# A fused four-layer kernel: TensorE's loops written out, and each scan state's own products set ahead of those with the state before it

## The chip, the cores and the metric

The kernel runs on one core of a Trainium2 chip, as one launch. The metric is the device time of that launch in microseconds. The engines are TensorE (PE: matmuls; PEld: its weight loads), VectorE (DVE), ScalarE (ACT), GpSimd (POOL) and SyncE (SP, which here only issues DMAs). They run their own instruction streams side by side and are held together by semaphores alone.

## The reference

Four layers with residual sums over `x` of 128 x 64 x 1024 (batch, channels, time), float32:

```
x = x + einsum('bct,bcd->bdt', x, W0[cond])                 # per-sample channel mix
x = x + mask1 * (causal_conv(x, K1) + x * D1)               # SSM layer 1
x = x + (x @ W2.T + bias) + scale * ((x @ A[id].T) @ B[id].T)   # 1024 x 1024 on the time axis, with adapters
m = mask3 * x
x = x + mask3 * (causal_conv(m, K3) + m * D3)               # SSM layer 3
# K[h, l] = 2 Re sum_n Ct[h, n] exp(dtA[h, n] * l),  l < 1024, 64 modes n per channel h
```

Since K is a sum of 64 complex modes, a causal convolution can be split: within a chunk of 256 steps it is a small Toeplitz product ("near"), and everything older reaches a chunk through a state of 128 real numbers for each channel and sample ("far"). The state behind chunk k is the chunk's own contribution plus the decayed state behind chunk k-1.

## The kernel before, in words

**Stages.** Stage 0 (about the first 240 us) loads x in four units `i` of two blocks of 128 time steps, makes the channel mix with float32 matmuls (line 618), and writes the result to a scratch in DRAM. Between its matmuls stand the transposes of the weights (602) and the sums for the convolution kernels (586). DVE and ACT take the sums out, SP issues the loads of x, ACT the stores.

Then come 16 groups `g` of four channels (heads `h`, HG = 4, NG = 16). Values are split into a high and a low float16 half, and each product is made of three matmuls: high x high, high x low, low x high. In `body(g, more1)` PE does, in this order: `stage2(g)` (lines 737 to 753, the 1024 x 1024 layer with the adapters), then, interleaved, the scan states and the first convolution of group g+1 (`states(0, g+1, k)`, `near1`, `far1`) and the scan states of the third layer of group g (`states(1, g, k)`), and last the third layer's convolution of group g (`near3`, `far3`). The last group has no group behind it and a shorter order.

**The states.** `states(v, g, k)` makes the sums of the state behind chunk k (k = 0, 1, 2) of layer v (0: first, 1: third) in one PSUM bank: for each of four heads six matmuls of 128 columns from the chunk's own values (line 675), and for k > 0 three more from the halves of the state behind chunk k-1 (line 679). ACT then makes the high half of the sum (`state_hi`, line 1055) and DVE the low half (`state_lo`, line 1457), with the semaphores `st_hi[v]` and `st_lo[v]`. Banks are 7, 6, 7 for v = 0 and 4, 5, 4 for v = 1, so k = 2 writes over the bank of k = 0. For k > 0 the waits for both halves and for the decay table (`v_lo`) stand ahead of all 36 matmuls of the state.

**What sets the order.** Everything is written out by hand in the order in which each engine's program stands; there is no scheduler. PE's program has two loops with a counter in a register: `Fori(1, NBLK // 2)` over units 1 to 3 of stage 0 (line 644) and `Fori(1, NG - 1)` over groups 1 to 14 (line 852). Unit 0 and groups 0 and 15 are written out. Inside a loop, semaphore targets that depend on the counter are computed by register instructions. The other engines have loops of their own and are not touched.

Other lines that the steps name: DVE's 1472 (`take_conv1`, the masked take-over of the first convolution), 1499 (`lowf`, the adapters' low-rank sums scaled) and 1502 (their low half), 1509 (`lo3`, low half of the third layer's input), 1557 (the masked take-over of the third layer), ACT's 1110 (`outt`, its sums taken out), POOL's 531 and 534 (`past_of`, the third layer's input put together again from transposed halves), 507 to 521 (`make_tables`).

Of the kernel before, what the change touches and what calls it, by code (L numbers as in the profile page):

```python
# [35 lines left out]
B, C, T = 128, 64, 1024  # L36
NBLK = T // P
# [9 lines left out]
HG = 4  # L47
NG = C // HG
TB = 16
CHUNK = TB * TB  # L50
NCH = T // CHUNK
# [16 lines left out]
def at_least(engine, semaphore, value):  # L68

    if not (isinstance(value, int) and value <= 0):  # L70
        engine.wait_ge(semaphore, value)


def build(nc, x, ids0, len1, ids2, len3, w0, ssm1, ssm3, w2, bias2, lora_a, lora_b, lora_s, out):
    with ExitStack() as ctx:
        def sem(name):
            return ctx.enter_context(nc.semaphore(name))
# [12 lines left out]
        ps = ctx.enter_context(nc.psum_tensor("ps", [P, 8, 512], F32))  # L90
# [86 lines left out]
        vd = (vd1, vd3)  # L177
        ut = (ut1, ut3)
        st = ((s1[:, 0], s1[:, 1]), (s3h, s3l))
# [97 lines left out]
        v_lo = sem("v_lo")  # L277
# [4 lines left out]
        st_hi = [sem(f"st_hi{v}") for v in range(2)]  # L282
        st_lo = [sem(f"st_lo{v}") for v in range(2)]
# [41 lines left out]
        def made(v, g):  # L325

            if v == 0:
                return 2 * g - 1 if isinstance(g, int) and g else (0 if isinstance(g, int) else 2 * g - 1)
            return 2 * NG - 1 if isinstance(g, int) and g == NG - 1 else 2 * g + 2
# [228 lines left out]
        def _(pe):  # L558
# [3 lines left out]
            for dgroup in range(8):  # L562
                for e in range(8):
                    for q in range(2):
                        mm = nc.tensor.matmul(ps[q * C:(q + 1) * C, dgroup, e * PAIRS:(e + 1) * PAIRS], src[:, 8 * dgroup + e, :],  # L565
                                              onehot[:, :].rearrange("i (n q) -> i q n", q=2)[:, q, :], start=True, stop=True)
# [39 lines left out]
            def stage0(i, first):  # L606
                for m in range(2 * STEPS):
                    n = 2 * STEPS * i + m
                    s = m % NXH
                    k, step, odd = m // STEPS, m % STEPS // 2, m % 2  # L610
                    blk = 2 * i + k
                    l = m // 2
                    if not odd:
                        pe.wait_ge(x_loaded[l % NXIN], 16 * (STEPS // NXIN * i + l // NXIN + 1))

                    at_least(pe, (s0_even_out, s0_odd_out)[odd], STEPS * i + m // 2 - 1)
                    for j in range(GPAIRS):
                        mm = nc.tensor.matmul(ps[:, s, j * P:(j + 1) * P], xin[:, l % NXIN, j, odd * P:(odd + 1) * P],  # L618
                                              pick[:, l * GPAIRS + j, :], start=True, stop=True)
                    mm.then_inc(s0_summed, 1)  # L620
                    if not odd:
                        continue
                    if first and k == 0:
                        if step == 1:
                            turn_params()
                        if step == 3:
                            turn_lot(LOT_A)
                        if step == 5:
                            turn_lot(LOT_B)
                    else:  # L630
                        if step == 2:
                            sum_k(blk - 1)
                        if first and step == 3:
                            turn_lot(LOT_W)
                        if first and step == 6:
                            turn_lot(LOT_W + 1)
                        if not first and k == 0 and step == 3:
                            turn_lot(blk + LOT_W, 0)
                        if not first and k == 0 and step == 7:
                            turn_lot(blk + LOT_W + 1, 1)  # L640

            pe.wait_ge(iota_done, 5)
            stage0(0, True)
            with pe.Fori(1, NBLK // 2) as i:
                stage0(i, False)
            pe.wait_ge(s0_even_out, NBLK * STEPS // 2)
            pe.wait_ge(s0_odd_out, NBLK * STEPS // 2)
# [4 lines left out]
            def states(v, g, k):  # L652

                bank = ((7, 6, 7), (4, 5, 4))[v][k]
                if k == 0:
                    pe.wait_ge(u_turned[v], 32 * (g + 1))
                    if v == 0:
                        pe.wait_ge(x1_hi, HG * (g + 1))
                        pe.wait_ge(x1_lo, HG * (g + 1))
                    else:  # L660
                        pe.wait_ge(x3_hi, NBLK * (g + 1))
                        pe.wait_ge(x3_lo, NBLK * (g + 1))
                else:
                    pe.wait_ge(st_hi[v], (NCH - 1) * g + k)
                    pe.wait_ge(st_lo[v], (NCH - 1) * g + k)
                    pe.wait_ge(v_lo, made(v, g) + 1)
                if v == 0 and k == 1:

                    at_least(pe, s2_out, NBLK * g)
                hi, lo = x_of[v]  # L670
                for h in range(HG):
                    o = ps[:, bank, h * B:(h + 1) * B]
                    for q, (part, xx) in enumerate([(0, hi), (0, lo), (1, hi)]):
                        for blk in range(2):
                            mm = nc.tensor.matmul(o, ut[v][:, part, 2 * h + blk, :], xx[:, h, 2 * k + blk, :],  # L675
                                                  start=(q == 0 and blk == 0), stop=(k == 0 and q == 2 and blk == 1))
                    if k:
                        for q, (part, ss) in enumerate([(0, 0), (0, 1), (1, 0)]):
                            mm = nc.tensor.matmul(o, vd[v][:, part, h, (2, 0)[v], :], st[v][ss][:, h, k - 1, :], start=False, stop=(q == 2))  # L679
                mm.then_inc(st_summed[v], 1)  # L680

            def near1(g, h):

                b0 = conv1_bank(g, h)
                early = isinstance(g, int) and g == 0
                if h == 0:
                    pe.wait_ge(g1_turned, g + 1)
                if early or h == 0:
                    pe.wait_ge(x1_hi, HG * g + h + 1 if early else HG * (g + 1))
                    pe.wait_ge(x1_lo, HG * g + h + 1 if early else HG * (g + 1))  # L690
                if early:

                    if h == 2:
                        pe.wait_ge(k_scaled, NBLK - 1)
                    if h == 3:
                        pe.wait_ge(c1_out, 1)
                elif h < 2:

                    at_least(pe, c3_out, HG * (g - 1))
                else:  # L700
                    pe.wait_ge(c1_out, HG * g + h - 1)
                for bank in range(2):
                    for d in range(2):
                        for q, (part, xx) in enumerate([(0, x1h), (0, x1l), (1, x1h)]):
                            o = ps[:, b0 + bank, :].rearrange("p (k b) -> p k b", k=4)
                            m = xx[:, h, 4 * bank:4 * bank + 4, :]
                            if d:
                                o = o.rearrange("p (k two) b -> p k two b", two=2)[:, :, 1, :]
                                m = m.rearrange("p (k two) b -> p k two b", two=2)[:, :, 0, :]
                            nc.tensor.matmul(o, g1[:, h, part, d * P:(d + 1) * P], m, start=(d == 0 and q == 0), stop=False)  # L710
# [110 lines left out]
            def body(g, more1):  # L821
                stage2(g)
                if more1:
                    states(0, g + 1, 0)
                    near1(g + 1, 0)
                    states(0, g + 1, 1)
                    near1(g + 1, 1)
                    states(1, g, 0)
                    states(0, g + 1, 2)
                    states(1, g, 1)  # L830
                    far1(g + 1, 0)
                    states(1, g, 2)
                    far1(g + 1, 1)
                    for h in range(2, HG):
                        near1(g + 1, h)
                        far1(g + 1, h)
                    for h in range(HG):
                        near3(g, h)
                        far3(g, h)
                else:  # L840
                    near3(g, 0)
                    states(1, g, 0)
                    near3(g, 1)
                    states(1, g, 1)
                    states(1, g, 2)
                    for h in range(HG):
                        if h >= 2:
                            near3(g, h)
                        far3(g, h)

            body(0, True)
            with pe.Fori(1, NG - 1) as g:
                body(g, True)
            body(NG - 1, False)


        @block.scalar
# [740 lines left out]
```

## Time and profile before

| | |
|---|---|
| median of 3 runs | 1691.71 us (1690.57 to 1693.37) |
| the profiled execution | 1686.25 us, its span 1684.4 us |
| mean granted TensorE clock | 0.978 of full speed |
| PE / PEld / DVE / ACT / POOL busy | 93 / 61 / 61 / 31 / 49% of the span |
| stage 0 and what precedes the groups | 0 to 279.7 us |
| 15 groups, 0 to 14 | 279.7 to 1597.0 us |
| the last group | 1597.0 to 1684.4 us |

The profile is of one execution. Its page gives busy times and shares; the trace behind it gives each instruction with the idle time of its engine ahead of it and what ended that idle time ("<-DVE gbuf L1457": a semaphore from DVE's line 1457; "<-issue": nothing that the profile can name). Matmuls are pipelined, so the duration of a merged row contains the latency of its last matmul (about 0.16 us), and the next row starts before it ends. Times in the rows are counted from the start of the span. Line numbers of rows are those of the kernel before.

### The profile page before, as it was taken

The numbers are of one execution on the slowest core, as the hardware profiler recorded it, in microseconds if no ns is written. First come the engines' busy times: TensorE is split into PE (matmuls) and PEld (weight loads), VectorE is DVE, ScalarE is ACT, GpSimd is POOL, SyncE is SP. The second block draws the span as 40 slices with busy tenths as digits, with TensorE's granted clock in tenths as the row PEclk, the third lists the DMA queues.
The fourth block names the chain that finished last, engine by engine and source line by source line (L and its number), as shares of the span: only waits on it lengthen the run. The fifth ranks groups of instructions, "written<-read, shape, count | busy, mean of one in ns | idle before, by whom it ended". The sixth has DMA issues, their size and how long they took to land.

```text
span 1684.4 us, 30702 instructions
## 1 busy us (share of the span) xinstructions
PE 1572.3 (93%) x12183; PEld 1028.3 (61%) x12183; DVE 1033.4 (61%) x1345; ACT 528.5 (31%) x674; POOL 822.0 (49%) x365
## 2 busy tenths in 40 slices
PE   6777767999999999999999999999999999999996
PEld 6776654474747475656566665656574747474744
DVE  7787775656575656565655565656566665656532
ACT  4444431332323232232323232323232323232211
POOL 2000032438292928384746556555556574738434
PEclk9989879999999999999999999999999999999998
DMA  7799957253534444352526253535352626262314
GB/s 226 270 353 338 359 206 198 44 129 83 100 102 93 107 87 122 72 137 59 150 47 158 52 141 68 137 72 137 67 142 52 147 52 142 67 142 62 83 47 100
DMA packets 425956, 216.82 MB, mean 129 GB/s; under 512 B 337144, under 2 KB 412416, under 8 KB 423872
## 3 DMA queue, kind: packets, MB, share of 16 engines
q1 hardware_dynamic: 409728, 176.67, 42.1%
q10 hardware_dynamic: 16192, 39.67, 6.4%
q8 instruction: 23, 0.38, 0.1%
q14 instruction: 13, 0.11, 0.0%
HBM read 94.19 MB, written 71.76 MB: 99 GB/s over the span
## 4 chain that ended last, share of the span: by engine, by line
PE 83%; DVE 7%; DMA 6%; issue 3%; ACT 1%; POOL 0%; POOLq 0%; DVEq 0%; SPq 0%; ACTq 0%
PE ps L745 39%; PE ps L784 7%; PE ps L675 7%; DMA arena<-in_x_dram 5%; PE ps L710 5%; PE ps L737 5%; PE ps L753 5%; PE ps L797 4%; PE ps L679 3%; PE ps L618 3%; PE ps L727 2%; PE ps L723 1%; PE ps L565 1%; DVE arena L1355 1%; DVE arena L1509 1%
## 5 line engine op out<-in xcount | busy, mean ns | idle before, releaser
L745 PE MATMUL ps<-arena,w2t 128*128 128x512 f16 x3072 | 681.3, 379 | 0.0
L745 PEld LDWEIGHTS ps<-arena,w2t 128*128 128x128 f16 x3072 | 300.4, 98 | 362.3
L531 POOL TENSOR_TENSOR arena<-arena 128x1024 f32<-128x1024 f16 x64 | 150.8, 2356 | 551.7 <-DMA arena<-arena 534.0
L1515 DVE TENSOR_SCALAR arena<-ps,biasx 128x512 f32<-128x512 f32 x128 | 94.4, 748 | 204.0 <-ACT arena L1079 203.8
L1079 ACT ACTIVATE arena<-ps,biasx 128x512 f16<-128x512 f32 x128 | 87.1, 687 | 421.1 <-PE ps L753 421.1
L507 POOL TENSOR_TENSOR arena<-arena 128x1024 f32<-128x1024 f32 x32 | 73.0, 2280 | 288.4 <-DMA arena<-tab_scratch 226.4
L618 PE MATMUL ps<-arena 128*128 128x128 f32 x1024 | 145.3, 305 | 49.1 <-DMA arena<-in_x_dram 27.1
L618 PEld LDWEIGHTS ps<-arena 128*128 128x128 f32 x1024 | 136.8, 217 | 55.4 <-issue 24.3
L710 PE MATMUL ps<-arena 128*128 128x512 f16 (+1 forms) x768 | 138.2, 331 | 8.1 <-DVE arena L1434 8.1
L784 PE MATMUL ps<-arena 128*128 128x256 f16 (+1 forms) x1536 | 138.4, 247 | 3.2 <-DVE arena L1509 3.0
L534 POOL TENSOR_TENSOR arena<-arena,one_xs 128x1024 f32<-128x1024 f32 x64 | 135.2, 2112 | 5.0
L1509 DVE TENSOR_TENSOR arena<-arena 128x512 f16<-128x512 f32 x128 | 136.0, 1073 | 0.0
L784 PEld LDWEIGHTS ps<-arena 128*128 128x128 f16 x1536 | 124.0, 98 | 14.4 <-issue 3.5
L1557 DVE COPY_PREDICATED arena<-past,arena 128x1024 f32<-128x1024 uint8 x64 | 91.5, 1432 | 59.5 <-POOL arena L534 42.3
L710 PEld LDWEIGHTS ps<-arena 128*128 128x128 f16 x768 | 74.8, 99 | 59.3 <-issue 11.4
L1465 DVE SCALAR_TENSOR_TENSOR arena<-gbuf,arena 128x1024 f16<-128x1024 f32 x64 | 104.7, 1637 | 1.2 <-ACT arena L1013 1.2
L675 PE MATMUL ps<-arena 128*128 128x128 f16 x1152 | 88.8, 220 | 13.5 <-DVE gbuf L1457 5.1
L517 POOL TENSOR_TENSOR arena<-arena 128x1024 f32<-128x1024 f32 x32 | 99.9, 3123 | 2.5
L753 PE MATMUL ps<-gbuf,bt 128*128 128x512 f16 x384 | 101.2, 379 | 0.0
L675 PE MATMUL ps<-arena,gbuf 128*128 128x128 f16 x1152 | 88.2, 220 | 8.5 <-issue 7.0
L1457 DVE SCALAR_TENSOR_TENSOR arena<-ps,arena 128x512 f16<-128x512 f32 x48 | 33.2, 692 | 96.5 <-ACT arena L1055 96.5
L737 PE MATMUL ps<-arena,at 128*128 128x512 f16 x384 | 87.6, 385 | 4.8 <-DVE arena L1477 4.8
(213 smaller groups left out, 2156.3 us busy)
## 6 DMA issues: line engine op xcount, KB each, us to landing
arena<-in_x_dram SPq DMA_DIRECT2D x64, 512.0 KB, 8.0
out_dram<-arena SPq DMA_DIRECT2D x64, 512.0 KB, 3.0
gbuf<-x_scratch SPq DMA_DIRECT2D x120, 256.0 KB, 3.7
arena<-krow_scratch SPq DMA_DIRECT2D x32, 512.0 KB, 4.5
x_scratch<-arena ACTq DMA_DIRECT2D x14, 1024.0 KB, 9.3
x_scratch<-arena ACTq DMA_DIRECT2D x14, 896.0 KB, 8.6
arena<-tab_scratch SPq DMA_DIRECT2D x32, 200.0 KB, 2.6
w2t<-in_L_cond_weight_dram ACTq DMA_DIRECT2D x8, 512.0 KB, 3.5
```

The lines of the kernel that those rows point to most:

```text
L517: ptt(v4, v4, m4, ALU.add).then_inc(v_made, 1)
L531: nc.gpsimd.tensor_tensor(past[:, h % 2].rearrange("p (k t) -> p k t", k=NBLK), x3t[:, h % 2, 0], x3t[:, h % 2, 1], ALU.add).then_inc(past ...
L534: nc.gpsimd.tensor_tensor(past[:, h % 2], past[:, h % 2], one_xs[:, :].to_broadcast([P, T]), ALU.mult).then_inc(past_ready, 1)
L618: mm = nc.tensor.matmul(ps[:, s, j * P:(j + 1) * P], xin[:, l % NXIN, j, odd * P:(odd + 1) * P], pick[:, l * GPAIRS + j, :], start=True, s ...
L675: mm = nc.tensor.matmul(o, ut[v][:, part, 2 * h + blk, :], xx[:, h, 2 * k + blk, :], start=(q == 0 and blk == 0), stop=(k == 0 and q == 2 ...
L710: nc.tensor.matmul(o, g1[:, h, part, d * P:(d + 1) * P], m, start=(d == 0 and q == 0), stop=False)
L737: mm = nc.tensor.matmul(ps[:, 7, :], at[:, part, k, :], xx[:, :, k, :], start=(k == 0 and q == 0), stop=(k == NBLK - 1 and q == 2))
L745: nc.tensor.matmul(ps[:, 4 + o % 3, :], w2t[:, o, part, k, :], xx[:, :, k, :], start=(k == 0 and q == 0), stop=False)
L753: mm = nc.tensor.matmul(ps[:, 4 + o % 3, :], bt[:, part, o * P:(o + 1) * P], xx, start=False, stop=(q == 2))
L784: nc.tensor.matmul(ps[:, bank, c0:c0 + n], xx[:, h, j, :], g3[:, h, part, g0:g0 + n], start=(j % 4 == 0 and xx is x3h and part == 0), stop ...
L1465: stt(x1l[:, h], x1f[:, h], XS / FS, x1h[:, h], ALU.mult, ALU.subtract).then_inc(x1_lo, 1)
L1509: tt(x3l[:, :, o, :], x3f[:, o % 2], x3h[:, :, o, :], ALU.subtract).then_inc(x3_lo, 1)
```

## The change

It touches PE's program alone, in three places. The loop over units 1 to 3 and the loop over groups 1 to 14 are written out, so that counters, branches and register instructions go and every semaphore target is a constant. In `states` the own products of all four heads now come first, and for k > 0 the waits for the halves of the state before and for the decay table stand behind them, ahead of the twelve matmuls that read them. For k = 2 a wait of its own stands ahead of the own products: that the low half of k = 0 was made, whose bank they write over. Since the four heads' sums are now open in one bank together, only the first matmul of a state has `start`. Matmuls, their number and their operands stay as they are.

```diff
             stage0(0, True)
-            with pe.Fori(1, NBLK // 2) as i:
+            for i in range(1, NBLK // 2):
                 stage0(i, False)
...
-                else:
-                    pe.wait_ge(st_hi[v], (NCH - 1) * g + k)
-                    pe.wait_ge(st_lo[v], (NCH - 1) * g + k)
-                    pe.wait_ge(v_lo, made(v, g) + 1)
+                elif k == 2:
+
+                    pe.wait_ge(st_lo[v], (NCH - 1) * g + 1)
                 if v == 0 and k == 1:
 
                     at_least(pe, s2_out, NBLK * g)
...
                             mm = nc.tensor.matmul(o, ut[v][:, part, 2 * h + blk, :], xx[:, h, 2 * k + blk, :],
-                                                  start=(q == 0 and blk == 0), stop=(k == 0 and q == 2 and blk == 1))
-                    if k:
+                                                  start=(h == 0 and q == 0 and blk == 0), stop=(k == 0 and q == 2 and blk == 1),
+                                                  skip_group_check=True)
+                if k:
+                    pe.wait_ge(st_hi[v], (NCH - 1) * g + k)
+                    pe.wait_ge(st_lo[v], (NCH - 1) * g + k)
+                    pe.wait_ge(v_lo, made(v, g) + 1)
+                    for h in range(HG):
+                        o = ps[:, bank, h * B:(h + 1) * B]
                         for q, (part, ss) in enumerate([(0, 0), (0, 1), (1, 0)]):
-                            mm = nc.tensor.matmul(o, vd[v][:, part, h, (2, 0)[v], :], st[v][ss][:, h, k - 1, :], start=False, stop=(q == 2))
+                            mm = nc.tensor.matmul(o, vd[v][:, part, h, (2, 0)[v], :], st[v][ss][:, h, k - 1, :], start=False,
+                                                  stop=(q == 2), skip_group_check=True)
                 mm.then_inc(st_summed[v], 1)
...
-            body(0, True)
-            with pe.Fori(1, NG - 1) as g:
-                body(g, True)
-            body(NG - 1, False)
+            for g in range(NG):
+                body(g, g < NG - 1)
```

On PE, in the loop over groups, `states(0, g+1, 1)` stands before like this (the semaphores that a matmul waits for are in brackets; `x6` means six alike; the six and three repeat for the other heads):

```order
L664 ISA
L666 REGISTER_ALU [waits st_lo0,st_hi0]
L71 REGISTER_ALU [waits v_lo]
L675 MATMUL ps<-arena 128x128 [waits s2_out]
L675 MATMUL ps<-arena 128x128 x5
L679 MATMUL ps<-gbuf,arena 128x128 x3
L675 MATMUL ps<-arena 128x128 x6
```

In the changed kernel the same state stands like this, and after "..." `states(1, g, 2)` (line 675 is 674 there, 679 is 684, and what follows them stands 6 lines further down):

```order
L674 MATMUL ps<-arena 128x128 [waits s2_out]
L674 MATMUL ps<-arena 128x128 x23
L684 MATMUL ps<-gbuf,arena 128x128 [waits v_lo,st_lo0,st_hi0]
L684 MATMUL ps<-gbuf,arena 128x128 x11
...
L674 MATMUL ps<-arena,gbuf 128x128 [waits st_lo1]
L674 MATMUL ps<-arena,gbuf 128x128 x23
L684 MATMUL ps<-arena,gbuf 128x128 [waits v_lo,st_lo1,st_hi1]
L684 MATMUL ps<-arena,gbuf 128x128 x11
```

The waits for the halves moved from ahead of the first own product to behind the 24th, and the register instructions are gone.

On PE, where unit 1 of stage 0 begins, before:

```order
L644 UNCONDITIONAL_BRANCH
L644 ISA
L71 ISA [waits x_loaded0]
L618 MATMUL ps<-arena 128x128 [waits s0_even_out]
L618 MATMUL ps<-arena 128x128 x3
```

and now:

```order
L618 MATMUL ps<-arena 128x128 x3
L618 MATMUL ps<-arena 128x128 [waits s0_even_out,x_loaded0]
L618 MATMUL ps<-arena 128x128 x3
L618 MATMUL ps<-arena 128x128 [waits s0_odd_out]
```

The branch is gone, and the wait for the loaded x is held by the matmul itself instead of by a register instruction. PE's program has 2483 matmuls before and 11415 now; what PE executes of them is the same.

## Rows read from the trace of the kernel before

**Rows 1.** The page, first part: busy time, share of the span, instructions.
```profile
PE 1572.3 (93%) x12183; PEld 1028.3 (61%) x12183; DVE 1033.4 (61%) x1345; ACT 528.5 (31%) x674; POOL 822.0 (49%) x365
```

**Rows 2.** Stretches of one lap each: stretch, length, PE busy (instructions), clock, DMA share, GB/s.
```profile
374.80:462.11 87.31, 86.46 (x663) 1.00 0.48 102
...
636.73:724.04 87.31, 86.46 (x663) 1.00 0.43 101
```

**Rows 3.** PE's waits over the whole span: who waited for whom, us, times, longest.
```profile
PE ps L618 <- DMA arena<-in_x_dram: 27.1, 10, 4.4
...
PE ps L675 <- issue: 10.4, 16, 3.4
...
PE ps L675 <- DVE gbuf L1457: 5.1, 14, 0.4
```

**Rows 4.** Timeline of PE, one group: start, us, line, tile, count [idle before, releaser].
```profile
426.60 1.50 PE L675 MATMUL ps<-arena 128*128 128x128 f16 x24
427.94 2.11 PE L710 MATMUL ps<-arena 128*128 128x512 f16 x12
430.43 0.51 PE L675 MATMUL ps<-arena 128*128 128x128 f16 x6 [0.38 <-DVE gbuf L1457]
...
439.76 0.50 PE L723 MATMUL ps<-gbuf,arena 128*128 128x128 f16 x6
...
441.38 0.49 PE L675 MATMUL ps<-arena,gbuf 128*128 128x128 f16 x6 [0.47 <-issue]
...
462.11 5.34 PE L737 MATMUL ps<-arena,at 128*128 128x512 f16 x24
```

**Rows 5.** Timeline of DVE in the same stretch.
```profile
429.38 0.69 DVE L1457 SCALAR_TENSOR_TENSOR gbuf<-ps,gbuf 128x512 f16<-128x512 f32 x1
...
436.57 0.69 DVE L1457 SCALAR_TENSOR_TENSOR arena<-ps,arena 128x512 f16<-128x512 f32 x1 [2.60 <-ACT arena L1055]
...
440.59 0.69 DVE L1457 SCALAR_TENSOR_TENSOR arena<-ps,arena 128x512 f16<-128x512 f32 x1 [1.32 <-ACT arena L1055]
```

**Rows 6.** Timeline of DVE, then of PE, early in the next group.
```profile
472.85 0.68 DVE L1499 TENSOR_TENSOR gbuf<-ps,adapter_scale 128x512 f32<-128x512 f32 x1
...
474.23 1.04 DVE L1502 TENSOR_TENSOR gbuf<-gbuf 128x512 f16<-128x512 f32 x1 [0.70 <-ACT gbuf L1072]
...
477.65 1.46 PE L753 MATMUL ps<-gbuf,bt 128*128 128x512 f16 x6
```

**Rows 7.** Timeline of PE ahead of the groups: `states(0, 0, 2)`, then `far1(0, 0)`.
```profile
265.13 0.49 PE L675 MATMUL ps<-arena 128*128 128x128 f16 x6 [1.46 <-ACT gbuf L1055]
...
268.81 0.49 PE L723 MATMUL ps<-gbuf,arena 128*128 128x128 f16 x6 [1.50 <-DVE gbuf L1457]
```

**Rows 8.** The chain that ended last, 230 to 345: start, us, what.
```profile
270.00 1.31 DVE gbuf L1472
...
279.68 7.42 PE ps L737 x24
```

**Rows 9.** Timeline of PE in the last group, then the chain that ended last.
```profile
1662.54 0.50 PE L675 MATMUL ps<-arena,gbuf 128*128 128x128 f16 x6 [1.46 <-ACT arena L1055]
...
1666.21 2.12 PE L797 MATMUL ps<-gbuf,arena 128*128 128x256 f16 x18 [1.50 <-DVE arena L1457]
...
1668.46 1.33 DVE arena L1557
1669.92 3.02 POOL arena L531
```

**Rows 10.** Stage 0 as one stretch: length, PE, PEld, DVE, ACT, POOL busy, clock, DMA share, GB/s.
```profile
30.00:240.00 210.00, 159.57 (x1334) 151.70 (x1335) 160.42 (x394) 91.29 (x158) 3.62 (x2) 0.90 0.90 318
```

**Rows 11.** The instruction queue: whole span; 374.80 to 462.11; 549.42 to 1596.96: packets, MB, share.
```profile
q8 instruction: 23, 0.38, 0.1%
...
q8 instruction: 5, 0.08, 0.4%
...
q8 instruction: 1, 0.02, 0.0%
```

## Predicted time

> **What bounds the kernel now.** I read the page's first part, then the stretches of one group each, then the list of PE's waits, then the timelines of single waits. PE is busy 93% of the span, no other engine over 61% [rows 1]. In a group of the steady part PE is busy 86.46 of 87.31 us at full clock, in the first lap of the loop as in the fourth [rows 2]. The matmuls and their count do not change, so only PE's idle time can go: 0.85 us a group, and what lies before and behind the groups.
>
> Whose waits are these? The list [rows 3] has 14 waits for DVE's L1457 (5.1 us) and 16 called "issue" (10.4 us, the longest 3.4). L1457 is the second half of a state. The timeline shows both in one group [rows 4]: PE is idle 0.38 us before 430.43, where `states(0, g+1, 1)` begins, and 0.47 us before 441.38, where `states(1, g, 2)` begins. DVE's rows [rows 5] explain them: the halves for the first are ready at 429.38 + 0.69 = 430.07, those for the second at 440.59 + 0.69 = 441.28, 0.10 us ahead of PE's start. So "issue" is a wait for DVE here too, and all 0.85 us stand ahead of a state with a predecessor, k = 1 or 2. One of the 16, 3.4 us, stands before the very first state, which the edit of the waits leaves alone; the other 15 make 10.4 - 3.4 = 7.0 us (groups 0 to 14, 0.47 each), and the 14 make 5.1 us (all laps, 0.36 each).
>
> **Part 1: own products first.** A state is 24 own products and 12 with its predecessor's halves. 24 own products take 427.94 - 426.60 = 1.34 us [rows 4], so 36 take 2.01 us and the 12 take 0.67. In the kernel before, all 36 stand behind the wait; now only the 12 do. In steady groups:
> - `states(0, g+1, 1)`: PE is free at 430.05 and has own work until 431.39; the halves come at 430.07. The wait ends 1.3 us before it is needed: all 0.36 us go.
> - `states(1, g, 2)`: PE is free at 440.91, own work until 442.25, halves at 441.28: all 0.47 us go, with 0.97 us over.
> - The other two of the group do not wait before and do not after.
>
> What is late next? The own products of k = 2 get a wait of their own (`st_lo` of k = 0, whose bank they overwrite). For v = 1 that half was made at 436.57 + 0.69 = 437.26 [rows 5], over 3 us ahead. The wait for `s2_out` stays before the own products of `states(0, g+1, 1)`; it is older than the half at 430.07, since DVE works in order. All in all a group has 86.46 us left, and nothing behind these states comes later than before: ACT and DVE take a state's sum when its last product is done, as now.
>
> Is another chain tied to the clock of the old period? The tightest I find is DVE's L1499, the scaled low-rank sums. Its input is ready when L737 is done, but DVE reaches it at 472.85, behind POOL's last product; its two steps end at 474.23 + 1.04 = 475.27, and PE needs them at 477.65 [rows 6]: 2.4 us of slack. That chain starts from work of the same group that PE releases (the transposes of x3 behind `x2_lo`, the sums of the second scan), which moves forward with PE, so the slack stays.
>
> Before the groups, `states(0, 0, 2)` waits 1.46 us and starts at 265.13; PE had been free since 263.67 [rows 7]. Own products now run from 263.67 to 265.01, the 12 others from 265.13 to 265.80 instead of 267.14: 1.34 us. The wait of 1.50 us behind it (L723) remains, for it starts from this state's end. The chain of work that ended last runs through here, by DVE's predicated copies to the first L737 [rows 8], so the 1.34 us reach the end. In the last group the same stands before `states(1, 15, 2)` at 1662.54: again 1.34 us, and the chain runs on through `far3` (after its 1.50 us wait), DVE's L1557 and POOL's L531 [rows 9]; POOL's third product starts at 1669.92, right behind DVE's copy for the first head (1668.46 + 1.33 = 1669.79), so it moves too. Sum of part 1: 5.1 + 7.0 + 1.3 + 1.3 = 14.8 us, rounded.
>
> **Part 2: loops written out.** PE's counting instructions and branches go. The lap's edge lies before L737 at 462.11, whose row shows no idle time [rows 4]: the branch costs nothing visible. A written count also makes waits shorter: with a register in between PE starts 0.36 us after DVE's end (430.43 - 430.07), without one ahead of the waiting matmul's own wait 0.10. In the steady groups this is within the 0.36 us already taken. In the units of stage 0 the waits for x are held by register instructions: 10 waits [rows 3] by 0.26 us bound that gain at 2.6 us. But there the DMA engines are busy 0.90 of the time at 318 GB/s and PE only 160 of 210 us [rows 10], and transfers, not PE, set the pace. The other bound is a loss, by instruction fetches (next).
>
> The code grows from 2483 to 11415 matmuls in PE's program (by the order). The instruction queue moved 0.38 MB in 23 packets [rows 11], so I estimate 0.38 MB / 2483 = 153 B a matmul if nearly all of it is PE's, and some 80 packets more. One occupies a DMA engine for 0.4% of 16 x 87.31 us / 5 = 1.1 us [rows 11]. In units 1 to 3, two copies of 304 matmuls are added, 6 packets: at most 6.7 us if all are exposed. I take 0 for stage 0, since its first unit, already written out, shows waits only for data, and keep -2.6 and +6.7 for the range. For the groups I take 0 too, and the trace has a good control: the lap from 374.80 to 462.11 fetches 5 packets, the twelve from 549.42 only 1 in all [rows 11], and both kinds take 87.31 us [rows 2]. The first group, written out in the kernel before, has no gap from its fetches either.
>
> A rule speaks for more gain here. The Trainium skill ("Runtime: NRT & Kernel Launch", section Instruction fetch mechanics) says that a taken branch whose target is outside the fetched window forces a fetch before execution goes on, a reason to prefer unrolling. The trace disagrees for this loop: laps without packets and no idle time at the edge. By the page the sum would be larger by a fetch for each edge; by the row it stays 14.8.
>
> **Against the profiled run:** span 1684.4, its time 1686.25 us; 1686.25 - 14.8 = 1671.5. The median of the runs shown is 1691.71, 5.5 us above the profiled one, and I predict in its terms: 1691.7 - 14.8 = 1676.9 us. A difference under 0.2% (3.4 us) can't be told from none.
>
> **The rivals.**
> - *The new fetches stall PE (slower).* Place: the stretch of states and convolutions behind stage 2, where a product takes 56 ns (1.34 us / 24), so that a packet (0.38 MB / 23 = 16.5 KB, about 108 matmuls by the estimate) lasts 6 us. If a packet queues that long behind the data of transfers, PE runs dry. It decides once more than 14.8 / 1.1 = 13 of the 80 packets are exposed. Two exposed in each of the 14 added groups cost 31 us: 1676.9 + 31 = 1708. Against it: the controls above, with the DMA engines at 0.48. Chance 5%.
> - *The gain is eaten by the next chain.* If the L1499 chain did not move with PE, its 2.4 us of slack would be used up after three groups; then only 2.4 + 2.7 us are won: 1686.6. Chance 7%.
> - *Branches cost more than rows show.* 13 edges between laps, 2 between units and 4 at entries and exits, at 1.1 us each, 21 us more: 1656. This is the page's rule above. Chance 4%: idle time at the edges would have to be missing from the trace.
> - *The change doesn't do what it says.* If PE's wait for the halves, now in mid-state, cost as much as before (0.85 us a group, say because it also holds back the loading of the next weights), time stays: 1691.7. Against it: waits already met stand in several places, as before L723, without a gap [rows 4]. Chance 4%.
>
> **How the numbers follow.** 80% for the forecast, 1676.9. Its range: down by the 2.6 us of stage 0 and 1.1 us of spread (median to lowest run), 1673; up by the 6.7 us of stage 0's fetches, less what the end loses or the runs scatter, 1683. The rivals lie outside and make the 20% left. Faster by over 0.2%: 80 + 7 + 4 = 91%; within 0.2%: 4%; slower: 5%.
>
> **What would show it.** Right: a group of 86.46 us at the same 86.46 busy, no idle row before a state's products in groups 1 to 14, 0.1 us left before the 12 products of `states(0, 0, 2)`, `far3` after its 1.5 us as before, and over 100 instruction packets. The registers: waits for x 0.1 to 0.3 us shorter each. Wrong: "issue" gaps of about 1 us inside L751 or the states at irregular places (fetches); a wait before L759 growing from group to group (the L1499 chain); a group shorter than 86.46 (the edges).

## The result: 1673.2 us, and a larger gain than forecast

The changed kernel took 1673.16 us (median of 4 runs, 1668.88 to 1673.52) against 1692.54 us for the kernel before beside it: a ratio of 0.988, interval 0.9861 to 0.9900. The forecast was a gain of 14.8 us from 1691.71, so 1676.9 us in a range from 1673 to 1683. The sign was right, the size was not: the medians differ by 19.4 us and the ratio gives 20.3, so that from 1691.71 the time would be 1672.3 or 1671.4, below the range. 1673.16 itself lies just inside, because the kernel before was 0.8 us slower in this comparison. A second measurement, below, gave a ratio of 0.9897 (0.9880 to 0.9914), a gain of 18.8 us between its medians.

The page of the profile after, first part and the instruction queue:

```profile
span 1671.3 us, 30319 instructions
...
PE 1568.8 (94%) x12183; PEld 1031.6 (62%) x12183; DVE 1046.6 (63%) x1345; ACT 530.3 (32%) x674; POOL 815.3 (49%) x365
...
q8 instruction: 96, 1.57, 0.4%
```

PE's busy time fell from 1572.3 to 1568.8 us [rows 1] though it executes the same matmuls. That is the first hint, no more, since these totals also hold what the clock does ahead of the laps and behind them: busy time was counted that no product needed. It shows in the stretches of one lap (length, PE busy, clock, DMA share, GB/s), the first and second after group 0, to be held against [rows 2]:

```profile
379.40:465.53 86.13, 86.13 (x662) 1.00 0.46 101
465.53:551.66 86.13, 86.13 (x662) 1.00 0.51 104
```

A lap takes 86.13 us and PE is busy in all of them; forecast were 86.46, with 86.46 busy. PE's timeline in one group, as in [rows 4]:

```profile
432.54 2.11 PE L716 MATMUL ps<-arena 128*128 128x512 f16 x12
434.49 1.50 PE L674 MATMUL ps<-arena 128*128 128x128 f16 x24
435.83 0.83 PE L684 MATMUL ps<-gbuf,arena 128*128 128x128 f16 x12
436.50 2.11 PE L716 MATMUL ps<-arena 128*128 128x512 f16 x12
438.45 1.50 PE L674 MATMUL ps<-arena,gbuf 128*128 128x128 f16 x24
...
443.81 0.50 PE L729 MATMUL ps<-gbuf,arena 128*128 128x128 f16 x6
444.15 0.82 PE L733 MATMUL ps<-gbuf,arena 128*128 128x256 f16 x6
444.80 1.50 PE L674 MATMUL ps<-arena,gbuf 128*128 128x128 f16 x24
```

No idle time stands before a state. And here is what was overlooked: L716 starts at 432.54 and its row lasts 2.11 us, to 434.65, yet the state starts at 434.49, 0.16 us before that end. In [rows 4] the same convolution starts at 427.94 with the same 2.11 us, and the state at 430.43, 0.38 us behind its end. From start to start that is 2.49 us against 1.95: 0.54 us, not 0.38.

Where did the time go between the two profiled executions? I cut both at the first product of each `stage2`:

| stretch | before | after | difference |
|---|---|---|---|
| up to the first product of `stage2(0)` | 279.68 | 285.84 | +6.2 |
| group 0 | 95.12 | 93.56 | -1.6 |
| groups 1 to 14 | 14 x 87.30 | 14 x 86.13 | -16.3 |
| the last group | 87.44 | 86.08 | -1.4 |
| span | 1684.4 | 1671.3 | -13.1 |

So two things had to be explained: 1.17 us a lap where 0.85 was idle, and 6.2 us lost ahead of the groups in the profile, which the medians of the runs don't show.

The -1.6 of group 0 is not the edit's alone. Its first 24 products, behind a wait of 4.80 us in both kernels, took 7.42 us before and 6.71 after, at mean granted clocks of 0.71 and 0.79. Without that row the group has 95.12 - 7.42 = 87.70 us before and 93.56 - 6.71 = 86.85 after. In the second execution of the changed kernel (`r_after` below) the group took 95.11 us with a first row of 8.03, which leaves 87.08. Between 87.70 and 87.08 lie the 0.6 us that one wait gives back; the other 0.9 us are the clock, at the group's start (0.7) and behind the wait of 3.46 us before `states(0, 1, 0)`.

### The profile page after: what moved, and what is told of

Same layout as the page of the kernel before. It is cut to its first block, busy times and chain, and to the rows that moved or that the text cites. A ratio compares the mean times of both kernels' runs of the same rounds, so it can differ in the third digit from the quotient of the medians.

```text
span 1671.3 us, 30319 instructions
## 1 busy us (share of the span) xinstructions
PE 1568.8 (94%) x12183; PEld 1031.6 (62%) x12183; DVE 1046.6 (63%) x1345; ACT 530.3 (32%) x674; POOL 815.3 (49%) x365
## 4 chain that ended last, share of the span: by engine, by line
PE 86%; DMA 6%; DVE 4%; issue 1%; POOL 1%; ACT 0%; POOLq 0%; SPq 0%; DVEq 0%; ACTq 0%
PE ps L751 40%; PE ps L674 8%; PE ps L716 7%; PE ps L790 7%; DMA arena<-in_x_dram 6%; PE ps L743 5%; PE ps L759 5%; PE ps L803 4%; PE ps L618 3%; PE ps L684 2%; PE ps L733 2%; PE ps L729 1%; PE ps L565 1%; DVE arena L1359 1%; POOL arena L531 1%
## 5 line engine op out<-in xcount | busy, mean ns | idle before, releaser
L531 POOL TENSOR_TENSOR arena<-arena 128x1024 f32<-128x1024 f16 x64 | 147.3, 2302 | 542.1 <-DMA arena<-arena 526.5
L507 POOL TENSOR_TENSOR arena<-arena 128x1024 f32<-128x1024 f32 x32 | 73.1, 2283 | 292.2 <-DMA arena<-tab_scratch 233.3
L618 PE MATMUL ps<-arena 128*128 128x128 f32 x1024 | 145.5, 304 | 53.3 <-DMA arena<-in_x_dram 31.7
L1513 DVE TENSOR_TENSOR arena<-arena 128x512 f16<-128x512 f32 x128 | 162.1, 1276 | 0.0
L716 PE MATMUL ps<-arena 128*128 128x512 f16 (+1 forms) x768 | 138.7, 332 | 8.2 <-DVE arena L1438 8.2
L790 PE MATMUL ps<-arena 128*128 128x256 f16 (+1 forms) x1536 | 138.8, 247 | 3.2 <-DVE arena L1513 3.0
L790 PEld LDWEIGHTS ps<-arena 128*128 128x128 f16 x1536 | 124.3, 99 | 14.6 <-issue 3.5
L534 POOL TENSOR_TENSOR arena<-arena,one_xs 128x1024 f32<-128x1024 f32 x64 | 130.0, 2031 | 5.0
L1561 DVE COPY_PREDICATED arena<-past,arena 128x1024 f32<-128x1024 uint8 x64 | 87.7, 1372 | 69.4 <-POOL arena L534 52.1
L716 PEld LDWEIGHTS ps<-arena 128*128 128x128 f16 x768 | 75.0, 99 | 59.8 <-issue 11.9
L517 POOL TENSOR_TENSOR arena<-arena 128x1024 f32<-128x1024 f32 x32 | 99.6, 3112 | 2.5
L1469 DVE SCALAR_TENSOR_TENSOR arena<-gbuf,arena 128x1024 f16<-128x1024 f32 x64 | 94.5, 1477 | 1.2 <-ACT arena L1017 1.2
L1476 DVE COPY_PREDICATED gbuf<-mask,ps 128x1024 f32<-128x1024 uint8 x64 | 83.2, 1301 | 13.8 <-issue 13.8
L1021 ACT ACTIVATE arena<-gbuf 128x1024 f16<-128x1024 f32 x64 | 67.5, 1055 | 74.5 <-DVE gbuf L1476 74.5
L509 POOL TENSOR_TENSOR arena<-arena 128x1024 f32<-128x1024 f32 x32 | 89.6, 2799 | 2.0 <-DVE arena L1454 2.0
```

The lines of the kernel that those rows point to most:

```text
L517: ptt(v4, v4, m4, ALU.add).then_inc(v_made, 1)
L531: nc.gpsimd.tensor_tensor(past[:, h % 2].rearrange("p (k t) -> p k t", k=NBLK), x3t[:, h % 2, 0], x3t[:, h % 2, 1], ALU.add).then_inc(past ...
L534: nc.gpsimd.tensor_tensor(past[:, h % 2], past[:, h % 2], one_xs[:, :].to_broadcast([P, T]), ALU.mult).then_inc(past_ready, 1)
L790: nc.tensor.matmul(ps[:, bank, c0:c0 + n], xx[:, h, j, :], g3[:, h, part, g0:g0 + n], start=(j % 4 == 0 and xx is x3h and part == 0), stop ...
L1469: stt(x1l[:, h], x1f[:, h], XS / FS, x1h[:, h], ALU.mult, ALU.subtract).then_inc(x1_lo, 1)
L1513: tt(x3l[:, :, o, :], x3f[:, o % 2], x3h[:, :, o, :], ALU.subtract).then_inc(x3_lo, 1)
```

## Experiments

Theory 1: a wait that empties PE costs its idle time and 0.16 us more, the latency of the last matmul, which the profile counts as busy. The rival: the additional gain is that of branches and register instructions. For the time ahead of the groups: either its written-out units are slower, or the profiled execution of the kernel before had a short stage 0 by chance.

### Loops alone: `e_loops`

The kernel before with both loops written out; `states` as it was.

```diff
-            with pe.Fori(1, NBLK // 2) as i:
+            for i in range(1, NBLK // 2):
...
-            body(0, True)
-            with pe.Fori(1, NG - 1) as g:
-                body(g, True)
-            body(NG - 1, False)
+            for g in range(NG):
+                body(g, g < NG - 1)
```

> Only the loops over units and groups are written out; the waits stand ahead of each state's own products as before. The changed kernel has laps of 86.13 us, 1.18 less than before, where the shown idle time was only 0.85. Theory 1 (a drain is not shown whole: each wait that empties PE also costs the latency of the last matmul, 0.16 us, which the profile counts as busy): laps of about 87.05, since only the 0.26 us of register instructions behind the wait of states(0, g+1, 1) go, PE busy still 86.46; the whole about 3.6 us under before. Theory 2 (the missing 0.33 us came from edges and register instructions): laps of 86.7 or less with PE busy 86.13, the whole 8 us or more under before.

Measured: 1690.38 us, ratio 0.9989 (0.9977 to 1.0001). Two laps:

```profile
381.65:468.69 87.04, 86.45 (x662) 1.00 0.47 100
468.69:555.73 87.04, 86.45 (x662) 1.00 0.51 102
```

Laps of 87.04 where theory 1 gave 87.05, and PE's busy time stayed at 86.45. The timeline shows what went:

```profile
434.79 2.11 PE L710 MATMUL ps<-arena 128*128 128x512 f16 x12
437.03 0.49 PE L675 MATMUL ps<-arena 128*128 128x128 f16 x6
```

The state starts 2.24 us behind the start of `near1` instead of 2.49: about the 0.26 us of register instructions behind the wait. Nothing of the lap's gain is left for the branches: 14 x 0.26 = 3.7 us is the whole yield of writing out the group loop. The run as a whole missed its forecast of 3.6 us: its median equals that of the kernel before (1690.37), and the interval of the ratio reaches from 3.9 us less to none. The laps did get shorter, so something outside of them gave time back; the units of stage 0, below, are the candidate.

### Own products alone: `e_own`

The changed kernel with both `Fori` loops put back (the diff above, the other way round).

> Only the own products are set first; both loops stay loops. Theory 1: laps of 86.13 us like the changed kernel's, PE busy 86.13, no idle time, the whole within 2 us of the changed kernel (ratio 0.988 to before). Theory 2: laps of 86.46, the whole 5 us behind the changed kernel.

Measured: 1670.60 us, ratio 0.9878 (0.9862 to 0.9895), the same as the changed kernel. Two laps, and the instruction queue:

```profile
372.58:458.71 86.13, 86.13 (x662) 1.00 0.45 104
458.71:544.84 86.13, 86.13 (x662) 1.00 0.44 103
...
q8 instruction: 23, 0.38, 0.1%
```

With loops, counters and 23 packets of code a lap takes 86.13 us, written out with 96 packets it takes 86.13 us. The order of the products is the whole gain of a lap; once it hides the waits, it hides the register instructions too. And the fetches that my slower rival feared cost nothing there.

### One wait put back at a time: `e_first01`, `e_first12`

The changed kernel with the three waits of one state back ahead of its own products (shown for the second; the first has `(0, 1)`).

```diff
+                elif (v, k) == (1, 2):
+                    pe.wait_ge(st_hi[v], (NCH - 1) * g + k)
+                    pe.wait_ge(st_lo[v], (NCH - 1) * g + k)
+                    pe.wait_ge(v_lo, made(v, g) + 1)
                 elif k == 2:
```

> The changed kernel with the three waits of states(0, g, 1) alone put back ahead of its own products. No register instruction stands behind them now, so PE should be shown idle 0.12 us there. Theory 1 (a drain hides the last matmul's latency, 0.16 us): laps of 86.41, 0.28 us over the changed kernel, PE busy 86.29, the whole 4 us over the changed kernel. Rival (cost is the idle time shown): laps of 86.25, 1.7 us in all.

> The changed kernel with the three waits of states(1, g, 2) alone put back ahead of its own products. Theory 1: idle 0.47 us shown, laps of 86.76 (0.47 + 0.16 over the changed kernel), PE busy 86.29, 9.5 us more in all and 1.3 us in the last group. Rival: laps of 86.60, 7 us in all.

Measured: 1676.43 and 1681.40 us, beside the changed kernel at 1670.58 on the same chip. One lap of each, `e_first01` first:

```profile
376.85:463.27 86.42, 86.30 (x663) 1.00 0.46 100
```

```profile
468.05:554.81 86.76, 86.29 (x662) 1.00 0.52 103
```

Forecast were 86.41 and 86.76. The whole is 5.9 us over the changed kernel in the first, where 4 were forecast, and 10.8 in the second, as forecast (9.5 and 1.3). In the first the wait costs 0.29 us a lap, of which only 0.12 is idle time; most of its price is in the busy column. The timeline of the second, at the wait:

```profile
446.04 0.82 PE L736 MATMUL ps<-gbuf,arena 128*128 128x256 f16 x6
447.33 1.50 PE L677 MATMUL ps<-arena,gbuf 128*128 128x128 f16 x24 [0.47 <-issue]
```

446.04 + 0.82 + 0.47 = 447.33. Without the wait (`L733` there is `L736` here) the next products start 0.65 us behind L733's start (444.15 to 444.80 above), here 1.29: 0.64 us more, not 0.47. Together the laps of all kernels:

| kernel | waits that empty PE | lap | PE busy | idle |
|---|---|---|---|---|
| before | 2 | 87.31 | 86.46 | 0.85 |
| `e_loops` | 2 | 87.04 | 86.45 | 0.59 |
| `e_first12` | 1 | 86.76 | 86.29 | 0.47 |
| `e_first01` | 1 | 86.42 | 86.30 | 0.12 |
| `e_own`, after | 0 | 86.13 | 86.13 | 0 |

Each wait adds 0.16 to 0.17 us to the busy time, whatever its idle time. That settles theory 1: the loops are not the cause, and each of the two waits, put back alone, brings its share back.

### Stage 0: `e_units`, `e_nounits`, `r_after`, `r_nounits`

`e_units` is the kernel before with only the unit loop written out. `e_nounits` is the changed kernel with only the unit loop kept. `r_after` and `r_nounits` are the changed kernel and `e_nounits` again, side by side.

```diff
-            with pe.Fori(1, NBLK // 2) as i:
+            for i in range(1, NBLK // 2):
```

> The kernel before with only the loop over units 1 to 3 of stage 0 written out. The changed kernel's profile had its first product of stage 2 6.2 us later than the kernel before's (285.8 against 279.7 us). Theory A (the profiled execution of the kernel before had a short stage 0 by chance, the form of the loop does not matter): ratio 1.000, within 2 us. Theory B (written-out units cost time by their instruction fetches between the transfers of x): 3 to 7 us slower, ratio 1.002 to 1.004.

> The changed kernel with the loop over the units of stage 0 kept as a loop. Theory A: as the changed kernel, ratio 0.988, within 2 us. Theory B: 3 to 7 us faster than the changed kernel, ratio 0.984 to 0.986.

> The changed kernel again, beside the next run on the same chip, to settle what writing out the units of stage 0 costs. Theory A (nothing): the same median as the next run within 1.5 us. Theory B (fetches between the transfers of x, or another pace of them): 2 to 5 us more than the next run.

> The changed kernel with the loop over the units kept, again. Theory A: ratio 0.988 as the changed kernel. Theory B: ratio 0.9855 to 0.987, 2 to 5 us under the run before it, and the first product of stage 2 earlier by as much.

`e_units` gave 1692.68 us, ratio 1.0010 (0.9998 to 1.0022), between the two theories; `e_nounits` 1668.78 us, 0.9864 (0.9848 to 0.9881). Both lean to written-out units being slower, neither clearly. The direct comparison does not confirm it: 1670.58 us (0.9897) against 1670.43 us (0.9895). The first product of `stage2(0)` in all profiles, those of the last two experiments included:

| units as a loop | units written out |
|---|---|
| before 279.7, `e_own` 277.6, `e_nounits` 282.5, `r_nounits` 282.7 | after 285.8, `r_after` 280.1, `e_loops` 286.3, `e_units` 287.4, `e_first01` 281.8, `e_first12` 286.9, `e_split` 282.2, `e_better` 281.7 |

The same kernel has 285.8 and 280.1 in two executions. Of these 5.8 us, 4.1 had arisen by the first product of `states(0, 0, 0)` (264.05 against 259.96), and 1.7 come behind it, where the 24 products of that state and the 12 of `near1` took 4.95 us at a granted clock of 0.66 in one and 3.29 at 1.00 in the other. So the place scatters by 5 us with the loop and by 7 written out, and the 6.2 us lie within that. But the two groups don't lie alike: their means are 280.6 and 284.0. The two ratios above lean the same way, and so do the 3.7 us that `e_loops` gained in its laps and did not show as a whole. So a cost of two or three microseconds of written-out units stays possible, though the direct comparison shows none; 6 us are excluded (the interval of `e_units` ends at 3.7).

### Further along the same path: `e_split`, `e_better`

The list of PE's waits in the changed kernel names what is left (the waits of stage 0 and of the first convolution, at its top, are not shown):

```profile
PE ps L743 <- DVE arena L1481: 4.8, 1, 4.8
PE ps L674 <- issue: 4.4, 1, 4.4
PE ps L674 <- DVE arena L1469: 3.5, 1, 3.5
...
PE ps L803 <- DVE arena L1461: 1.5, 1, 1.5
```

`e_split` takes the third: ACT and DVE split group 1's x1 one step earlier within group 0.

```diff
-                    if isinstance(g, int) and g == 0 and o >= HG:
-                        x1_split_lo(1, o - HG)
+                    if isinstance(g, int) and g == 0 and HG - 1 <= o < NBLK - 1:
+                        x1_split_lo(1, o - HG + 1)
```

`e_better` adds two moves in PE's order.

```diff
             near1(0, 1)
+            near1(0, 2)
             pe.wait_ge(w2_hi, LOT_W + NBLK)
...
             states(0, 0, 0)
-            near1(0, 2)
...
                     states(1, g, 0)
-                    near3(g, 1)
                     states(1, g, 1)
                     states(1, g, 2)
+                    near3(g, 1)
```

> The changed kernel with the splits of group 1's x1 made one step earlier in group 0 (behind outputs 3 to 6 instead of 4 to 7, on ACT and DVE). The 3.46 us wait before states(0, 1, 0) should go. Theory 1: 3.46 + 0.16 us, and the stretch at half clock behind it as well, 1 to 2 us (states(0, 1, 0) took 2.72 us for 24 products there, 1.50 elsewhere; near1 2.38 instead of 2.11): 4.5 to 6 us less in group 0, whose length falls from 93.6 or 95.1 (both occur in runs so far) to about 89.5. Rival (DVE falls behind earlier in the group and PE waits for s2_out there): group 0 stays over 93 us.

> The same, and near1(0, 2) moved ahead of states(0, 0, 0), where PE waits 3 to 4.4 us for the transposes of the first bases, and near3(15, 1) moved behind states(1, 15, 2), where it covers the halves of that state. Theory 1: 1.95 us of products go into the first gap, against one short wait of 0.2 + 0.16 us between states(0, 0, 0) and (0, 0, 1); the last group loses the wait of 1.5 + 0.16 us and gains two of 0.2 + 0.16: 1 us. Together about 2.5 us below the run before it, 7 to 8 below the changed kernel, ratio 0.984 to 0.986 to the kernel before.

Measured beside the kernel before at 1690.17 us: `e_split` 1666.26 us, ratio 0.9853 (0.9830 to 0.9875); `e_better` 1661.57 us, ratio 0.9833 (0.9816 to 0.9849), where 0.984 to 0.986 were forecast. Group 0 took 89.74 us in `e_split`, about as forecast. Without its first 24 products that is 81.79 us against the 87.08 of `r_after`, 5.3 less: 3.46 + 0.16 for the wait and 1.65 for products that ran at the low clock behind it. In `e_better` the group took 88.44 us; the 1.3 us between them lie in the group's first 24 products again (7.95 and 6.66 us), which neither move touches. Ahead of the groups the move of `near1(0, 2)` did what it was meant to: from the first product of `near1(0, 0)` to that of `stage2(0)` it is 281.69 - 253.36 = 28.33 us, in `e_split` 282.20 - 252.18 = 30.02, so 1.7 us less where 1.95 - 0.36 = 1.6 were forecast. The last group fell from 86.08 to 83.55 us, by 2.5 instead of 1.0. `e_better`'s timeline there:

```profile
1630.95 2.14 PE L790 MATMUL ps<-arena 128*128 128x256 f16 x24 [3.04 <-DVE arena L1513]
1632.93 2.84 PE L674 MATMUL ps<-arena,gbuf 128*128 128x128 f16 x48
1635.89 0.83 PE L684 MATMUL ps<-arena,gbuf 128*128 128x128 f16 x12
...
1638.85 2.14 PE L790 MATMUL ps<-arena 128*128 128x256 f16 x24
1640.83 2.13 PE L803 MATMUL ps<-gbuf,arena 128*128 128x256 f16 x18
```

The wait before L803 is gone, as meant. More than half of the 2.5 us is the clock: in the changed kernel the first L790 took 3.79 us for the same 24 products, 1.65 more, which leaves 0.9 for the move.

```profile
1640.23 3.79 PE L790 MATMUL ps<-arena 128*128 128x256 f16 x24 [3.04 <-DVE arena L1513]
```

The granted clock over those ten microseconds is 0.83 there and 1.00 in `e_better`, behind the same wait of 3.04 us. The kernel before and `e_units` differ in the same way, though their last groups are the same program: the first L784, behind 3.04 us too, took 3.36 us in one and 2.14 in the other, and the last group 87.44 and 85.80 us. So the low clock behind such a wait comes in some executions and not in others, and I don't count it as a gain of the reordering. The two moves are worth 1.7 + 0.9 = 2.6 us by the rows; the medians differ by 4.7, and the rest is not explained beyond this scatter.

## Why the prediction was off, step by step

**What bounds the kernel, and which waits:** right. Only PE's idle time could go, "issue" before `states(1, g, 2)` was a wait for DVE's half, and both waits went.

**Part 1, steady groups:** the mechanism was right and the term mis-sized. The failed step is "all in all a group has 86.46 us left"; measured were 86.13. I took PE's busy time for the time that its products need, and PE as free at 430.05, the end of a merged row, although I had written of the rows myself that they contain 0.16 us of latency at their end. The last matmul of a row is shown 0.16 us longer than it holds up the next one; while PE streams, this tail lies under the next product, and when a wait empties PE it stands alone, as busy time. Two such tails a lap make 86.46 - 86.13 = 0.33 us, 14 x 0.33 = 4.6 us. With them the sum is 16.3 (laps, measured) + 0.6 (group 0: 0.47 + 0.16) + 1.3 + 1.4 = 19.6 us; the medians give 19.4 and, in the second measurement, 18.8. The runs scatter by more than these differ, so that a match to 0.2 us is luck. The Trainium skill ("Perfetto Trace Analysis", section Summary: the profiler window per engine type) says that a TensorE row ends at an estimated end; the rows here agree in so far as the shown end lies 0.16 us behind the point where the next row can start.

**Part 1, ahead of the groups and in the last:** right. `states(0, 0, 2)`'s last twelve products start after a gap of 0.12 us, and the wait of 1.51 us behind them stayed:

```profile
271.01 1.50 PE L674 MATMUL ps<-arena 128*128 128x128 f16 x24
272.63 0.83 PE L684 MATMUL ps<-gbuf,arena 128*128 128x128 f16 x12
274.97 0.49 PE L729 MATMUL ps<-gbuf,arena 128*128 128x128 f16 x6 [1.51 <-DVE gbuf L1461]
```

From `far1`'s start back to where `states(0, 0, 2)` can begin it is 274.97 - 271.01 = 3.96 us; before it was 268.81 - 263.51 = 5.30 ([rows 7]; 263.51 is 0.16 us ahead of the 263.67 that I used), 1.34 less. The last group lost 1.36 us, with the clock low for as long in both profiles: from the first product of `near3(15, 0)` to that of `near3(15, 1)` it is 4.96 us before and 4.97 after.

**Part 2:** right for the groups. The 0.26 us of register instructions exist (`e_loops`), and as I said they lie within the wait that goes anyway. Branches cost nothing that a lap shows: `e_own` keeps them and has the laps of the written-out kernel, with 23 packets in all. The Trainium skill ("Runtime: NRT & Kernel Launch", section Instruction fetch mechanics) has a taken branch force a fetch when its target is outside the fetched window; the traces show no such fetch at the edges of this loop, 1 packet in twelve laps. The code grew to 96 packets, 73 more (I had estimated 80, and over 100 in all), without a gap in the laps. For stage 0 my 0 may be wrong by a few microseconds of loss; the runs don't decide it. The waits for x did not get shorter as I had said: they sum to 25.8 to 30.0 us in the four profiles with the loop over units and to 29.0 to 31.7 in the eight without. The "two copies of 304 matmuls" behind the 6.7 us are a slip: of the 11415 - 2483 = 8932 matmuls added, 13 laps of 660 make 8580, which leaves 176 for each unit, and `e_units` fetched 5 packets more, not 6.

**The profiled execution against the median:** I carried its 5.5 us of difference over as a constant. That profile's stage 0 is one of the shorter ones among twelve, which would account for the difference; no second profile of that kernel was taken to show it. It did no harm here, since the sum was taken against the median, but a single profile of the changed kernel alone would have shown 13 us of gain, and for a wrong reason close to my 14.8.

**The rivals:** none occurred, though one sign of being wrong did: "a group shorter than 86.46 (the edges)". The group was shorter and the edges were not the cause, so the sign was badly chosen. The slower rival is refuted by equal laps with and without fetches, the L1499 chain moved with PE (laps stay at 86.13 to the end, 1205.8 us for 14), the edges are refuted by `e_own`, and a wait in mid-state that costs as much as before by the laps without idle time. The range was too narrow on its low side, since it had a lower bound for stage 0 and for the scatter but none for the main term, which I took as exact.

## What to carry to other kernels

When a wait empties PE, count from the start of one product to the start of the next and compare with the same pair in a place without a wait: here each short wait cost about 0.16 us more than its idle time, and one of 0.12 us idle cost 0.29. Work that does not need the awaited value belongs ahead of the wait, even if it has to be split from work on the same sum; writing out the group loop by itself gave 0.26 us a lap, and nothing once the waits were covered. Before a profile's stage times are compared between two kernels, look how far the same kernel's stages scatter.

## What was not expected of the hardware

Two register instructions between the waits for the halves and the matmul behind them cost 0.26 us a time (laps of 87.31 against 87.04), but only as long as PE was waiting there (86.13 with and without them once it was not). A loop body of 660 matmuls ran lap after lap almost without fetching its code again: 1 packet in twelve laps [rows 11]. Writing it out meant 5 to 6 packets a lap at no cost in time.
